# A scan, attention and FP4 kernel: new order of the first chunk, the last half and the FP4 tail

## The reference

```python
x = x + mamba(_layernorm(x))        # conv of 4 taps, SiLU, scan over the sequence
x = x + moe(_layernorm(x))          # two rounds, top 2 of 8 experts
x = x + attention(_layernorm(x))    # 6 layers, as 8 sequences of 256 tokens
x = x + ffn_fp4(_layernorm(x))

# mamba, the part ahead of the scan and its step
dt = softplus(einsum('blr,dr->bld', x_dbl[..., :8], dt_proj_w) + dt_proj_b)
dA = exp(dt_t[..., None] * A)
h = h * dA + (dt_t * x_t)[..., None] * B_t[:, None, :]
y = einsum('bds,bs->bd', h, C_t)

# one attention layer
w_avg = softmax(scores, axis=-1).mean(axis=1)
new_w = softmax(w_avg + rel[None], axis=-1)
h1 = _ln(h + einsum('blm,bme->ble', new_w, h), l1w, l1b)
h2 = _ln(h1, l2w, l2b)
ff = relu(h2 @ w1.T + b1_) @ w2.T + b2_
h = _ln(h2 + ff, l3w, l3b)

# the FP4 block: both operands of each product are quantized in blocks of 16
scale = maximum(max(abs(xb)) / 6.0, 1e-12)
q = GRID[searchsorted(MID, abs(xb / scale))] * sign(xb) * scale
h = silu(fp4_linear(x, w_gate)) * fp4_linear(x, w_up)
out = fp4_linear(h, w_down)
```

## Time and profile before

| what | us |
| --- | --- |
| three timed executions | 2735.45, 2740.74, 2745.2 |
| their median | 2740.74 |
| the profiled execution, whole | 2755.81 |
| its span (first to last instruction) | 2754.0 |
| first scan starts (L1168) | 47.83 |
| last exponential's sum ends | 2622.6 |
| VectorE busy over the span | 2422.1 (88%) |
| PE busy | 2356.9 (86%) |
| ScalarE busy | 2297.2 (83%) |
| GpSimd busy | 1562.0 (57%) |

### The profile page before, as it was taken

The page is one execution under the profiler, slowest core; times in us unless marked ns, Lnnn a source line. Parts: engine busy times, 40 slices in busy tenths (PEclk is TensorE's granted clock), DMA queues, the critical chain, the costliest instruction groups (busy, mean ns, idle before and its releaser), DMA issues.

```text
span 2754.0 us, 93639 instructions
## 1 busy us (share of the span) xinstructions
PE 2356.9 (86%) x38225; PEld 1248.3 (45%) x38225; DVE 2422.1 (88%) x3331; ACT 2297.2 (83%) x4208; POOL 1562.0 (57%) x2959
## 2 busy tenths in 40 slices
PE   5777576799999998999989998999999999899846
PEld 3444365344444444444444444444444444444435
DVE  4888744799999999999999999999999999999956
ACT  5888533599999999999999999999999999999832
POOL 4879764535664466544664456644665446643564
PEclk8888888799999999999999999999999999999977
DMA  3222223311101111011110111101010111100000
GB/s 95 78 92 73 69 77 84 90 48 51 45 29 39 49 47 43 25 48 42 54 36 32 48 35 57 35 37 48 31 54 31 48 43 37 35 33 11 2 1 16
DMA packets 52140, 127.22 MB, mean 46 GB/s; under 512 B 6017, under 2 KB 40705, under 8 KB 47233
## 3 DMA queue, kind: packets, MB, share of 16 engines
q1 hardware_dynamic: 43329, 113.12, 12.3%
q0 software_dynamic: 2432, 5.08, 0.6%
q10 hardware_dynamic: 5952, 3.04, 0.4%
HBM read 96.09 MB, written 29.18 MB: 45 GB/s over the span
## 4 chain that ended last, share of the span: by engine, by line
PE 35%; issue 19%; POOL 17%; DVE 12%; ACT 12%; DMA 1%; POOLq 0%; SPq 0%; ACTq 0%; DVEq 0%; another core or an unknown queue 0%
PE bank L708 11%; PE bank L777 11%; PE bank L788 9%; ACT E L1048 9%; DVE NM L1417 8%; POOL hC L1553 2%; POOL acc L1659 2%; POOL H L1669 1%; ACT acc L999 1%; POOL smp L1652 1%; POOL H L1672 1%; PE bank L689 1%; POOL hC L1556 1%; POOL dg L1717 1%; PE bank L702 1%
## 5 line engine op out<-in xcount | busy, mean ns | idle before, releaser
L1417 DVE TENSOR_REDUCE NM<-bank 128x1 f32<-128x1024 f32 x1536 | 1799.6, 1208 | 73.2 <-PE bank L777 52.5
L1048 ACT ACTIVATE E<-bank,NM 128x1024 f32<-128x1024 f32 x1536 | 1707.4, 1118 | 161.6 <-DVE NM L1417 135.8
L777 PE MATMUL bank<-KS,QS 72*32 72x512 bf16 x12288 | 957.3, 387 | 161.9 <-ACT E L1048 112.4
L788 PE MATMUL bank<-E,dg 128*32 128x256 f32 x12288 | 924.6, 385 | 1.7 <-ACT acc L999 1.7
L1717 POOL TENSOR_TENSOR dg<-mask,RZ 128x128 f32<-128x128 f32 x384 | 152.9, 398 | 823.9 <-DVE RZ L1427 728.1
L777 PEld LDWEIGHTS bank<-KS,QS 72*32 72x32 bf16 x12288 | 251.8, 96 | 706.9 <-ACT E L1048 592.6
L788 PEld LDWEIGHTS bank<-E,dg 128*32 128x32 f32 x12288 | 384.7, 111 | 290.2 <-issue 60.9
L1048 ACT ACTIVATION_READ_ACCUMULATOR E<-bank,NM 128x1 f32 x1536 | 310.7, 202 | 0.0
L1659 POOL TENSOR_TENSOR acc<-acc,rel 128x256 f32<-128x256 f32 x384 | 272.2, 729 | 7.8 <-ACT acc L999 7.8
L708 PE MATMUL bank<-H,ET 128*32 128x129 f32 x6144 | 189.3, 275 | 6.3 <-DVE ET L1360 6.3
L708 PE MATMUL bank<-hT,WL 128*32 128x256 f32 x2304 | 164.0, 388 | 26.3 <-ACT UB L1010 22.0
(11 more groups left out here) (261 smaller groups left out, 2679.4 us busy)
## 6 DMA issues: line engine op xcount, KB each, us to landing
QS<-scratch SPq DMA_DIRECT2D x69, 384.0 KB
KS<-scratch SPq DMA_DIRECT2D x22, 1152.0 KB
scratch<-UB SPq DMA_DIRECT2D x144, 128.0 KB
CB<-crows SPq DMA_DIRECT2D x32, 512.0 KB, 3.8
WL<-in_wl SPq DMA_DIRECT2D x6, 1091.0 KB, 21.4
KS<-scratch SPq DMA_DIRECT2D x6, 384.0 KB
first<-in_fill SPq DMA_DIRECT2D x8, 247.5 KB, 4.2
second<-in_fill SPq DMA_DIRECT2D x8, 247.5 KB, 4.1
```

The source lines that it names most:

```text
L777: inst = PE_.matmul(bank[x % 3][32 * i:32 * i + 32, k * 512:k * 512 + 512], QS[0:72, half % 2, 4 * hq + i, r0:r0 + 32], KS[0:72, b, k, 4 * ...
L788: inst = PE_.matmul(pb(6)[32 * k:32 * k + 32, 256 * grp:256 * grp + 256], dg[:, x // 4 % 3, x % 4, :], E[:, x % NE, :].rearrange("p (i k c ...
L1048: A_.activation(E[:, x % NE, :], bank[x % 3][:, :], ACT.Exp, bias=NM[:, x % 4:x % 4 + 1], accum_out=ZS[:, quad % 3, j:j + 1]).then_inc(s[" ...
L1417: V.tensor_reduce(NM[:, x % 4:x % 4 + 1], bank[x % 3][:, :], AX.X, ALU.max, negate=True).then_inc(s["rowmax"], 1)
```

## The change

Four parts are changed; the arithmetic of the middle of the attention stage is not.

**The first chunk.** Chunk 0 gets a list of its own, `FIRST`. VectorE makes two of the four `WX` products, which GpSimd made alone. The dt rows' product (`xpdt`) stands between `z0` and `z1`, and the C rows' product behind the dt products. Softplus goes by halves (one channel group of 128 each): abs, exp and ln on ScalarE, the relu part as a VectorE max with 0 (`fmax`), and `U` on VectorE (`fu`) instead of GpSimd. A one-element exp (`warm`) stands ahead of the first abs. C and B rows are copied behind the logarithms, and the decays of the first two steps (`dec`) ahead of the copies of `UT`.

**The last two halves.** Half 22 has a table `NEAR_DUE`, in which its third norm's pieces stand at steps 37 to 42. For half 23 the new `END_DUE` places all pieces at steps 7 to 13, and its norms are made by `end_norm_dve`: VectorE takes statistics, the variance, the subtraction with the gain (`na`) and the scaling with the offset (`nb`); GpSimd makes only the power (`pw`, L1753 of the new file). `xb` (L1756, GpSimd) adds the third norm's offset to x ahead of time, so that `nb2` adds straight to x and `fin` goes. Norm 2's result is written to the layer's `H` tiles, and each `h2t` transpose waits for its own tile instead of for the whole norm.

**The quantization in seven operations.** The correction by 1 - 2^-22 is taken into the scaled product, as a scalar_tensor_tensor (L1489 of the new file). This holds for all groups and for the two weights, `wq03` and `wq13` go.

**The last hidden group.** In `qh7` VectorE makes all of the second tile's quantization, and GpSimd requantizes the first tile alone. Its last transpose waits for VectorE's part.

The diff, cut to its core. Of the new tables `LAST` only two lines are shown, since the rows below tell its order; of `READY`'s pieces the waits that count one more (`k + 2` for `k + 1`) are left out.

```diff
+FIRST = {"PE": "trx conv0 conv1 conv2 conv3 conv4 conv5 conv6 conv7 z0 xpdt z1 dtp0 dtp1 xpc btp utp0 utp1",
+         "ACT": "xt silu0 silu1 silu2 dr silu3 warm fabs0 fexp0 fabs1 fexp1 fln0 fln1 crow bt dec0 dec1 ut0 ut1",
+         "DVE": "bn var xn wx fmax0 fone0 fmax1 fone1 fsum0 fu0 fsum1 fu1",
+         "POOL": "pow xa res"}
...
-    return [(k, x) for at in sorted(READY[engine]) for x in READY[engine][at].split()]
+    return [(k, x) for x in FIRST[engine].split()]
...
+END_DUE = {"PE": {(8, "g"): "h2t", (8, "h"): "ff1_00 ff1_01", (9, "h"): "ff1_10 ff1_11",
+                (10, "g"): "ff1_20 ff1_21", (10, "h"): "ff1_30 ff1_31", (11, "h"): "ff2_0 ff2_1 ff2_2 ff2_3",
+                (12, "h"): "ff2_4 ff2_5 ff2_6 ff2_7"},
+           "ACT": {(8, "a"): "h2c", (8, "b"): "re0", (9, "b"): "re1", (10, "a"): "re2", (10, "b"): "re3"},
+           "DVE": {(7, "e"): "nv0 na0 nb0", (8, "m"): "bn10 bn11 bn12 bn13 nv1 na1 nb1",
+                (11, "m"): "add2 bn20 bn21 bn22 bn23 nv2 na2", (12, "m"): "nb2"},
+           "POOL": {(7, "f"): "pw0", (8, "f"): "pw1", (11, "d"): "hb0 hb1", (11, "f"): "xb", (13, "f"): "pw2"}}
...
-        places = END_DUE if half == HALF_N - 1 else HALF_DUE
+        places = END_DUE if half == HALF_N - 1 else NEAR_DUE if half == HALF_N - 2 else HALF_DUE
...
+            elif p == "warm":
+                A_.activation(tiny[0:1, 2:3], tiny[0:1, 0:1], ACT.Exp)
+            elif p[:4] == "fabs":
+                c = int(p[4])
+                e.wait_ge(s["dtp"], c + 1)
+                A_.activation(E1[:, c, :], pb(BANKS[f"dtp{c}", k][0]), ACT.Abs, bias=c_("dt_b", c, 1)).then_inc(s["dt_abs"], 1)
+            elif p[:4] == "fexp":
+                c = int(p[4])
+                e.wait_ge(s["dt_abs"], c + 1)
+                A_.activation(E1[:, c, :], E1[:, c, :], ACT.Exp, scale=-1.0).then_inc(s["dt_exp"], 1)
+            elif p[:3] == "fln":
+                c = int(p[3])
+                e.wait_ge(s["dt_one"], c + 1)
+                A_.activation(E2[:, c, :], E2[:, c, :], ACT.Ln).then_inc(s["dt_ln"], 1)
+            elif p[:3] == "dec":
+                c = int(p[3])
+                if c == 0:
+                    e.wait_ge(s["early"], 2)
+                e.wait_ge(s["dt_sum"], c + 1)
+                A_.activation(dA[:, c, :], DT[:, 0, c, :], ACT.Exp, scale=Aneg[:, c * 16:c * 16 + 1]).then_inc(s["decay"], 1)
...
+                    if p >= 2:
+                        A_.activation(dA[:, p % 4, :], DT[:, k % 2, c, :], ACT.Exp, scale=Aneg[:, c * 16 + st_:c * 16 + st_ + 1]).then_inc(s["decay"], 1)
...
+                for j in range(2, 4):
+                    V.tensor_tensor(WX[:, j, :], WX[:, j, :], w_("in_proj", 0, 256), ALU.mult).then_inc(s["wx"], 1)
+            elif p[:4] == "fmax":
+                c = int(p[4])
+                e.wait_ge(s["dt_abs"], c + 1)
+                own.count(V.tensor_scalar(DT[:, 0, c, :], pb(BANKS[f"dtp{c}", k][0]), c_("dt_b", c, 1), 0.0, ALU.add, ALU.max))
+            elif p[:4] == "fone":
+                c = int(p[4])
+                e.wait_ge(s["dt_exp"], c + 1)
+                own.then(V.tensor_scalar(E2[:, c, :], E1[:, c, :], 1.0, None, ALU.add))
+                V.scalar_tensor_tensor(E1[:, c, :], E2[:, c, :], 1.0, E1[:, c, :], ALU.subtract, ALU.subtract).then_inc(s["dt_one"], 1)
+            elif p[:4] == "fsum":
+                c = int(p[4])
+                e.wait_ge(s["dt_ln"], c + 1)
+                e.wait_ge(s["dt_one"], c + 1)
+                own.then(V.tensor_tensor(E2[:, c, :], E2[:, c, :], E1[:, c, :], ALU.subtract))
+                V.tensor_tensor(DT[:, 0, c, :], DT[:, 0, c, :], E2[:, c, :], ALU.add).then_inc(s["dt_sum"], 1)
+            elif p[:2] == "fu":
+                c = int(p[2])
+                e.wait_ge(s["dt_sum"], c + 1)
+                e.wait_ge(s["silu"], c + 1)
+                V.tensor_tensor(U[:, c, :], DT[:, 0, c, :], XS[:, c, toks(0)], ALU.mult).then_inc(s["dt_x"], 1)
...
+        def end_norm_dve(e, own, n, p):
+            a, k = n % 2, int(p[2])
+            var = smp[:, a, k, :, :]
+            src, dst = (ZA[:, a], ZA[:, a], HB)[k], (ZA[:, a], next_h(n), HB)[k]
+            gain, offset = (wl(n // 4, "ln", 256 * k + 128 * i, 128) for i in range(2))
+            if p[:2] == "nv":
+                if k == 0:
+                    e.wait_ge(s["tbn0"], 4 * n + 4)
+                    own.count(V.scalar_tensor_tensor(var[:, :, 3], ZW[:, a, :, 128], EPS / 4.0, ZW[:, a, :, 128], ALU.mult, ALU.mult))
+                else:
+                    e.wait_ge(s["tbn"], 8 * n + 5 * k - 1)
+                for t in range(4):
+                    own.count(V.bn_aggr(var[:, t, 0:2], st[:, a, k, t, :]))
+                e.wait_ge(own.sem, own.n)
+                if k == 0:
+                    V.tensor_tensor(var[:, :, 2], var[:, :, 1], var[:, :, 3], ALU.add).then_inc(s["tbn0"], 1)
+                else:
+                    V.tensor_scalar(var[:, :, 2], var[:, :, 1], EPS, None, ALU.add).then_inc(s["tbn"], 1)
+            elif p[:2] == "na":
+                for t in range(4):
+                    own.count(V.scalar_tensor_tensor(dst[:, t, :], src[:, t, :], var[:, t, 0:1], gain, ALU.subtract, ALU.mult))
+            else:
+                e.wait_ge(own.sem, own.n)
+                e.wait_ge(s["tpow"], 3 * n + k + 1)
+                for t in range(4):
+                    r = n // 2 % 2 * 8 + 4 * (n % 2) + t
+                    out, more = (X[:, r, :], X[:, r, :]) if k == 2 else (dst[:, t, :], offset)
+                    inst = V.scalar_tensor_tensor(out, dst[:, t, :], var[:, t, 3:4], more, ALU.mult, ALU.add)
+                    if k == 0:
+                        own.count(inst)
+                    elif k == 1:
+                        inst.then_inc(s["add1"], 1)
+                    elif t == 3:
+                        inst.then_inc(s["fin"], 1)
+
+        def post_dve(e, own, n, p):
+            if p[:2] in ("nv", "na", "nb"):
+                end_norm_dve(e, own, n, p)
+                return
             if p in ("part1", "part3"):
...
-            elif i == 3:
-                inst = V.tensor_scalar(rs, rs, 1.0 - 2.0 ** -22, None, ALU.mult)
             elif i == 4:
-                inst = V.tensor_tensor(v3(x), v3(src), rs.unsqueeze(2).to_broadcast([128, n // 16, 16]), ALU.mult)
+                inst = V.scalar_tensor_tensor(v3(x), v3(src), 1.0 - 2.0 ** -22, rs.unsqueeze(2).to_broadcast([128, n // 16, 16]),
+                                              ALU.mult, ALU.mult)
...
-                    fp4_dve(e, own, i, src, n, QA[:, k, 0:n], QP[:, k, 0:n], QC[:, k, 0, 0:n // 16], QC[:, k, 1, 0:n // 16], s["cut"])
+                x, c, sc = QA[:, k, 0:n], QP[:, k, 0:n], QC[:, k, 0, 0:n // 16]
+                for i in (0, 1, 2, 4, 5, 6) + (7,) * (p != f"qh{NG - 1}"):
+                    fp4_dve(e, own, i, src, n, x, c, sc, QC[:, k, 1, 0:n // 16], s["cut"])
+                if p == f"qh{NG - 1}":
+                    e.wait_ge(own.sem, own.n)
+                    e.wait_ge(s["ht"], GT * (j - 2) + GT)
+                    w0, w1 = slice(0, I_), slice(I_, 2 * I_)
+                    V.tensor_tensor(x[:, w0], x[:, w0], c[:, w0], ALU.add).then_inc(s["cut"], 1)
+                    own.then(V.tensor_tensor(x[:, w1], x[:, w1], c[:, w1], ALU.add))
+                    own.then(V.tensor_tensor(x[:, w1], x[:, w1], c[:, w1], ALU.subtract))
+                    V.tensor_tensor(HQ[:, j % 2, 1, :].rearrange("p (n k) -> p n k", k=16), x[:, w1].rearrange("p (n k) -> p n k", k=16),
+                                    sc[:, NBL:2 * NBL].unsqueeze(2).to_broadcast([128, NBL, 16]), ALU.mult).then_inc(s["cut"], 1)
...
+                    e.wait_ge(s["tbn"], 8 * n + 5 * k)
+                G.tensor_tensor(smp[:, a, k, :, 3], smp[:, a, k, :, 2], mhalf[:, 0:4], ALU.pow).then_inc(s["tpow"], 1)
```

82 lines of the change are left out of this document (53 added, 29 removed), and 36 rows, old and new, of tables (END_DUE, LAST).

## The result

The changed kernel takes 2716.57 us (median of four, 2713.94 to 2717.48), the kernel before 2740.2 (median of four, 2735.45 to 2745.2). The ratio is 0.9913, with a 95% interval of 0.9901 to 0.9925: 24 us less, where 30 were forecast. The profiled execution of the changed kernel has a span of 2712.1 us, 41.9 less than the earlier trace rows. Not all of that difference is the change's: 15.7 us of it lie between the last scan and the first row maximum of attention (165.5 us in the profile of before, 149.9 after), where no edit reaches.

What follows compares the result with a forecast made beforehand. Attention was taken as bound by VectorE, head and tail as chains of waits. Gains 8.5 + 0.7 + 4.9 + 15.1 = 29.2, called 30 for a possibly larger head lead; 2740.7 - 30 = 2711 us, range 2698 to 2726.

Steps and rivals of the forecast that it cites:

- The head, 8.5 us: Up to the first scan: shortening this chain of waits moves everything behind it 8.5 us earlier.
- The thin cover: C rows' store and first load end near 38, 3 us before the first product; losing this costs 1 or 2 us.
- larger lead of ScalarE: Behind the first scan: ScalarE's second set of copies starts 10.2 us earlier, so between 8.5 and 10 arrives.
- The rival that the lead is absorbed: In the scans: GpSimd sets the pace and the head's lead is lost; 21 us gained in all, 2720; chance 0.05.
- The quantization in attention, 0.7: Weights' quantization in attention: two fewer VectorE instructions save 0.7 us, between 0.3 and 1.
- The scaling, 1.5: Tail's 12 quantization groups: dropping one operation saves 1.5 us, not 5.4, since the product would wait in its place.
- The tail's first part, 4.9: Up to the first FP4 group of hidden rows: earlier x group and norms on VectorE gain 4.9 us.
- The tail's second part, 15.1: From the first hidden group to the end: 91.6 us become 76.5, a gain of 15.1 us.
- The last tile, 0.4 to 1.8: Behind the last VectorE group: splitting two tiles between GpSimd and VectorE gains 0.4 us if they exclude each other, otherwise 1.8.
- paid twice: In the tail: GpSimd and VectorE exclude each other, groups stay at 5.7, norms at 11; 17 gained, 2724; chance 0.12.
- packs better: In the tail: norms 7.7, groups 4.6, gate and up 2.5; 38 us gained with the head, 2703; chance 0.15.
- Slower than before: Behind the last softmax: VectorE and GpSimd exclude each other wherever both work on SBUF rows; 2750; chance 0.03.

Runs made afterwards that it cites:

- the head alone: The kernel before with only the first chunk's new order added; 2751.48 us beside 2759.19 for the kernel before, ratio 0.9972.
- the tail alone: The changed kernel with the first chunk put back as before; 2741.34 us beside 2759.19 for the kernel before, ratio 0.9945.
- the last kernel: The changed kernel with the last norm's power behind both requantizations and the last groups' gate products earlier; 2726.51 us beside 2755.59 before, ratio 0.9888.

## Why the prediction was right, point by point

The direction and the range (2698 to 2726) held; the point, 2711, was 5.6 us too low, and the gain 24 instead of 30. The main mechanisms held as well: a shorter chain of waits at the head, and norms that leave GpSimd's chain at the end. One of the signs that the prediction itself named as wrong did appear: norm rows of over 0.5 us each. In three of the six sets of four norm rows the mean was over that (2.06, 2.94 and 6.28 us for four).

**The head, 8.5 us: right, as a sum and in its steps.** The first scan came 8.16 earlier, and alone the head is worth 7.7 (0.9972). By steps, forecast and measured: conv starts 10.4, 10.39; conv's part 0.9, 0.7 (its end 20.90 to 20.20); DR ends 23.3, 23.58; the logarithm ends 30.9, 31.08; from there to the last U 3.6, 3.71; the scan starts 39.3, 39.67. The thin cover, the C rows' store and load, held: the first product that reads them starts at 42.10, right behind the scan ahead of it. No run shows the larger lead of ScalarE, for which 0.8 was added to the sum: of 8.16 at the first scan 7.7 are found at the last (344.6 to 336.9), but over all profiles the stretch between the two takes 293.8 to 298.2 us, so one pair of profiles can't show 1 us either way.

**The rival that the lead is absorbed** fell with the same rows and with the head alone.

**The quantization in attention, 0.7:** can't be told. From the first exponential to the last one's sum it is 2110.9 us before and 2111.0 after, and 2110.4 to 2115.3 over all kernels.

**The scaling, 1.5: the right mechanism, mis-sized.** The rows of before had said that most of the operation's time is waiting that would move to the next one. It does, but the two operations together wait a little more than one: 2.8 us by the means, 2.4 by VectorE's busy time.

**The tail's first part, 4.9: measured 6.7** (from the last exponential's sum to the first hidden group 40.1 and 33.4). The walk in it was close: first group of x forecast 8.7 behind the start of the tail, measured 8.6; h2's transposes forecast 25 behind, measured 23.2 to 24.4. The two norms on VectorE were put at 11 us because of GpSimd; from 2611.97 to 2623.42 they take 11.4. What was too high was PE's and ScalarE's way to the first SiLU.

**The tail's second part, 15.1: measured 11.9** (91.6 and 79.7). This is the step that was off in size, by 3.2 us. Its sum was VectorE 64.3, gaps 3.3, end 8.9. Term by term, forecast and measured: add2 and the last norm 7.2 and 9.7; the gaps ahead of the gate products 3.3 and 4.9 (0.20, 0.66, 3.37, 0.66); the end 8.9 and 9.3; and the other way, the hidden groups 39.2 and 38.3, their products 7 and 6.7, the groups of x 9.4 and 9.2. So the largest miss is the last norm. The forecast had seen that its power holds up the requantizations, and had asked who waits for those, but not what the two requantizations then do to the four norm rows that start at the same moment. They take 6.28 instead of 1.14, 5.1 us more; the 7.2 had room for half of that.

**The last tile, 0.4 to 1.8: measured 1.4 to 1.9.** The exclusion is there (1.13 and 0.99 for rows of 0.52), but the first tile's transposes now overlap the second tile's rows, which the bound of 0.4 left out. The 8.9 in the sum goes with the upper bound of 1.8 and not with the lower one: before, the same end (from the start of L1406, 2743.26) took 10.7 us. The end measured 9.3, 0.4 more than the sum had.

**The rival "paid twice"** had the right mechanism and the wrong extent: 5.1 us at the third norm's rows, 0.9 and 1.8 at the first norm's (2.06 and 2.94 instead of 1.13), 1.9 in the last group of x (5.57 against 3.65) and 0.5 to 0.6 in four hidden groups (5.06 to 5.17 against 4.54), but no group at its 5.7. **The rival "packs better"** needed gate and up in 2.5 and norms at 7.7; neither came (4.16 and 11.4). **Slower than before** would have needed an overlap of under 10 us; VectorE's 92.6 and GpSimd's 56.4 lie in 113.0, an overlap of 36 at least.

**The base.** The forecast took 30 off the median and not off the profiled execution, though the reason that it gave was only that the latter is one execution. That was the right choice by luck. The profile of before has the long stretch between the scan and attention (165.5 us) that two groups have, which alone is worth the 15 us; that its timed executions had the short one is argued from their median (2740.2, like the 2739.23 of the group with the short stretch) and not shown, since they left no trace. Taken off the profiled execution, the forecast would have been 2726, 9 us too high. And had the change been read out of the two profiles, 41.9 us would have been credited to it.

**From 26.8 in the traces to 24 in the times.** The head (8.2) and the tail (18.6) of the two profiles give 26.8. The tail of the changed kernel isn't always 113.0: with the same order and the same instructions it is 113.1, 114.3 and 116.9 in three other profiles, and the PE's busy time in it goes with that (69.0, 69.0, 71.1 and 75.7). The forecast's 29.2 without the 0.8 stands against these 26.8: the tail was 1.4 too hopeful (20.0 and 18.6, its first part 1.8 better and its second 3.2 worse than forecast), the head 0.3, and the 0.7 of the weights' quantization isn't found.

## What to carry to other kernels

When work is moved from GpSimd to VectorE, write down for each moved row which GpSimd row runs at that moment, not only which row waits for it: in this kernel a VectorE row with two SBUF inputs that met a requantization row lasted as long as that row (1.5 to 1.8 us instead of 0.34), while GpSimd's power did it no harm. Then ask who uses the time that an order sets free: taking the requantizations out of the norm's way freed 4.6 us of VectorE and shortened the part behind add2 by 1.3, until the gate products were put ahead as well. A step that is a chain of waits (the head) could be forecast to a few tenths from its rows, by ending each piece at the engine that releases the next; a step in which two engines share a resource could not. Two profiles from different chips must be compared stage by stage before their difference is called the change's.

## What the runs showed of the hardware

**The same tail is longer where the PE's granted clock is lower.** Four profiles of the same tail order and instructions: the tail in us, with PE's busy time and its granted clock as the profile's columns have them. The changed kernel on a second chip, the changed kernel without the early load (both whole tails; PE is the third column, the clock the third from the end):

```profile
2610.40:2723.50 113.10, 68.97 (x589) 50.70 (x589) 92.61 (x201) 35.36 (x98) 56.36 (x62) 0.86 0.04 10
```

```profile
2613.00:2729.90 116.90, 75.68 (x589) 54.98 (x589) 92.60 (x201) 35.49 (x98) 56.36 (x62) 0.77 0.03 10
```

The first profile has 113.0 at 0.86 too, the tail alone 114.3 at 0.84. VectorE's busy time is the same in all (92.6 to 92.7), and the PE's is 6.7 us longer in the longest; that the 3.8 us of tail come from it is the natural reading, but no run holds the rest fixed. Other orders give other lengths at a like clock: 113.0 at 0.79 with the power behind both requantizations, 109.0 at 0.84 for the last kernel. Before, the tail was 131.6 at 0.78 and 131.3 at 0.79, two profiles only. What decides the clock of an execution in this stretch, no run shows.

**One VectorE row between two GpSimd rows.** Where GpSimd works requantization rows one after the other, VectorE's rows with two SBUF inputs go one by one between them (four rows in 6.28 us beside four GpSimd rows of 1.38 to 1.72). Beside GpSimd's power on 128x4 (1.04 us) four such rows took 1.13, as with GpSimd idle. A row of VectorE with one SBUF input can be held too: in the kernel with the power behind, the tensor_scalar on 128x4 that follows the statistics took 1.19 instead of 0.17, while GpSimd's L1820 ran until 2645.4:

```profile
2644.26 1.19 DVE L1414 TENSOR_SCALAR smp<-smp 128x4 f32<-128x4 f32 x1
```

**The experts' stage has two lengths,** some 135 and 155 us, with the same instructions; in the three groups, one chip each, it went with the group.
